# A graph layer and a gated FFN on one core: GpSimd's gathers without a readback, a head that VectorE does alone, and an order planned with other prices

## The reference

```
x = x + gnn(layernorm(x), src, dst, rel)
x = x + ffn(layernorm(x))

gnn:  S = feat[src];  for r in 0, 1: h = relu(relu(S W_r^T + b_r) W_r^T + b_r)    # the one of the edge's relation
      agg = segment_sum(msgs, dst)
      i, g, o of agg W_ih^T + b_ih + b_hh (4 parts, f unused)
      c = sigmoid(i) tanh(g);  hn = sigmoid(o) tanh(c)
      relu(relu(hn W1^T + b1) W2^T + b2) W3^T + b3
ffn:  weights = x wr + br;  the 1561 nodes of highest weight get  (gelu(x w1 + b1) w2 + b2) * weight
      the result of it is added to x for those nodes, for the others x alone
```

## Time and profile before

| | us |
|---|---|
| median of 3 runs | 752.13 |
| lowest, highest | 749.86, 757.51 |
| the profiled execution: its time | 752.0 |
| its span, first to last instruction | 750.2 |
| TensorE busy | 668.3 (89%) |
| VectorE busy | 411.4 (55%) |
| GpSimd busy | 445.9 (59%) |
| ScalarE busy | 234.5 (31%) |

### The profile page before, as it was taken

One profiled execution on the slowest core, in us unless ns is written; L12 is line 12 of the kernel. 1 busy time (PEld: TensorE's weight loads), 2 busy tenths in 40 slices (PEclk: granted clock), 3 DMA queues, 4 the chain that ended last, 5 costly groups with the idle time before them and its releaser, 6 DMA issues.

```text
span 750.2 us, 9583 instructions
## 1 busy us (share of the span) xinstructions
PE 668.3 (89%) x3037; PEld 433.4 (58%) x3037; DVE 411.4 (55%) x1280; ACT 234.5 (31%) x403; POOL 445.9 (59%) x1301
## 2 busy tenths in 40 slices
PE   3978959689999999994857999999999999699986
PEld 2665638456666666653423666565665665377665
DVE  6764987898887988841215035143053244314475
ACT  1243234244333333300312333423414233032601
POOL 3567870376767676767777677647257677760000
PEclk9999979799999999997978999999999999799999
DMA  9300111333323333337333333313123332330005
GB/s 278 95 32 28 56 56 57 98 100 91 104 87 105 89 105 88 97 98 253 94 95 99 92 98 88 94 52 102 44 62 102 91 99 84 107 91 22 1 1 171
DMA packets 37881, 67.63 MB, mean 90 GB/s; under 512 B 7951, under 2 KB 25376, under 8 KB 37824
## 3 DMA queue, kind: packets, MB, share of 16 engines
q0 software_dynamic: 17712, 48.39, 22.0%
q1 hardware_dynamic: 19296, 17.77, 7.3%
q10 hardware_dynamic: 816, 0.79, 0.3%
HBM read 57.17 MB, written 9.75 MB: 89 GB/s over the span
## 4 chain that ended last, share of the span: by engine, by line
PE 75%; DVE 12%; POOL 6%; issue 3%; DMA 2%; ACT 2%; SPq 0%; DVEq 0%; POOLq 0%
PE BIG L1253 21%; PE SM L1397 12%; PE SM L1322 11%; PE AG L1416 10%; PE BIG L1384 6%; POOL ring L1046 5%; PE BIG L1212 4%; PE SM L1223 3%; PE BIG L1276 3%; PE AG L1223 2%; PE BIG L1193 2%; DVE half_b L1530 1%; DVE late L1514 1%; DVE ve L1484 1%; DMA ring<-message_table,rowT 1%
## 5 line engine op out<-in xcount | busy, mean ns | idle before, releaser
L1046 POOL DMA_INDIRECT ring<-message_table,rowT x369 | 366.3, 993 | 158.0 <-issue 106.1
L1416 PE MATMUL AG<-ring,onehot 128*128 128x512 f16 x369 | 95.3, 393 | 29.1 <-DMA ring<-message_table,rowT 25.2
L1322 PE MATMUL SM<-half_b,late 128*128 128x256 f32 x400 | 94.1, 383 | 1.5 <-DVEq L1598 0.8
L1322 PEld LDWEIGHTS SM<-half_b,late 128*128 128x128 f32 x400 | 74.5, 190 | 18.9 <-issue 5.7
L1253 PE MATMUL BIG<-fT,half_a 128*128 128x512 f32 (+1 forms) x192 | 81.4, 579 | 0.0
L1416 PEld LDWEIGHTS AG<-ring,onehot 128*128 128x128 f16 x369 | 41.5, 115 | 67.1 <-DMA ring<-message_table,rowT 16.6
L1253 PE MATMUL BIG<-half_b,half_a 128*128 128x512 f32 (+2 forms) x200 | 73.0, 521 | 0.5 <-ACT half_b L1135 0.5
L1397 PE MATMUL SM<-late,half_a 128*128 128x512 f16 x250 | 70.1, 381 | 0.7 <-ACT half_a L1119 0.7
L1767 DVE TENSOR_TENSOR onehot<-dst,iota_b 128x512 f16<-128x512 f16 (+3 forms) x115 | 45.0, 422 | 43.9 <-PE AG L1416 42.7
L1635 DVE TENSOR_TENSOR late<-late 128x1024 f32<-128x1024 f32 (+2 forms) x7 | 7.8, 1112 | 103.0 <-ACT late L1140 103.0
L1723 DVE TENSOR_SCALAR oh_key<-iota,lists 128x350 f16<-128x350 f16 (+8 forms) x228 | 58.8, 315 | 4.6 <-PE BIG L1384 4.0
(11 more groups left out here) (194 smaller groups left out, 909.8 us busy)
## 6 DMA issues: line engine op xcount, KB each, us to landing
ring<-message_table,rowT POOLq DMA_INDIRECT x369, 2.8
message_table<-late SPq DMA_DIRECT2D x10, 512.0 KB, 3.6
out<-X SPq DMA_DIRECT2D x24, 128.0 KB
X<-in_x SPq DMA_DIRECT2D x4, 512.0 KB, 6.2
half_a<-in_f SPq DMA_DIRECT2D x1, 1024.0 KB, 7.7
half_b<-in_f SPq DMA_DIRECT2D x1, 1024.0 KB, 12.0
message_table<-late SPq DMA_DIRECT2D x2, 384.0 KB, 2.9
half_a<-in_w_ih_t SPq DMA_DIRECT2D x1, 768.0 KB, 4.3
```

Source lines behind the costliest of these rows:

```text
L1046: nc.gpsimd.indirect_dma_start(ring[:, to * W:(to + 1) * W], None, table, bass.IndirectOffsetOnAxis(ap=rowT[:, t:t + 1], axis=0)).then_inc ...
L1322: last = nc.tensor.matmul(bank, hidden_of(s)[:, c, j * P:(j + 1) * P], F2[:, c, :], start=(c == 0), stop=(c == HC - 1))
L1416: mm = nc.tensor.matmul(AG[w % 2][:, :], hot[:, :, i], ring[:, to:to + W], start=(c == FIRST_OF[w] and i == lo), stop=(c == LAST_OF[w] and ...
```

## The change: what it does

- The pauses are gone: GpSimd issues its 369 gathers and waits only for places in the ring. `land` has no term for them.
- Of the head, GpSimd keeps the memsets of the tile constants, in eight batches that wait on the progress of the table and of the layer norms in place of the bias sums, in another order (tile_low first). VectorE takes over the slot rows (`rows_of_slots`, 47 operations after group 1) and the test of the bounds (`compare`, after group 4), which compares tile by tile and reduces a maximum, in place of differences formed on GpSimd. The slot products on TensorE come after group 3, not 4.
- The addition of b3 to X leaves the head (two groups on VectorE, five on GpSimd) and is done by VectorE at the start of `gates(s)`, for each s.
- Seven keys and the rows ahead of them are made before the last group's messages (`EARLY`); the slots of the key ring are renumbered so that these seven lie outside the memory that the messages use.
- TensorE's wait for the whole table moves from ahead of the hot phase to the first dense product and the first visit.
- aggT starts its bank with its first product, without a product of zeros ahead of it.
- The planner's prices are others.

```diff
-    BURST = 7
-    PAUSES = list(range(BURST, NQ, BURST))
...
-                    begin = max(landed[-1] if landed else 120.5, waited[k - RQ] + 3.0 if k >= RQ else 0.0)
-                    landed.append(begin + 1.25 * quad_tiles(k) + (3.0 if k in PAUSES else 0.0))
+                    begin = max(landed[-1] if landed else 126.1, waited[k - RQ] + 3.0 if k >= RQ else 0.0)
+                    landed.append(begin + 1.25 * quad_tiles(k))
...
                 if kind == "tile":
-                    return sum(max(0.06, 0.02 + (hi - lo) * A / 2400) for _, lo, hi in HALVES[s])
+                    return sum(max(0.05, 0.005 + (hi - lo) * A / 2400) for _, lo, hi in HALVES[s])
                 if kind == "dense":
-                    return 0.218 * len(piece(s[1]))
+                    return 0.2145 * len(piece(s[1]))
                 if kind == "down":
-                    return 0.24 * len(down_parts(s[0])[s[2]])
+                    return 0.43 * len(down_parts(s[0])[s[2]])
...
-                return {"aggT": 0.3, "gates": 1.4, "W1": 0.24, "W2": 0.12, "W3": 0.24, "n2T": 0.25, "F1": 0.24}[kind] * nb
+                return {"gates": 2.6, "W1": 0.43, "W2": 0.22, "W3": 0.43, "n2T": 0.27, "F1": 0.43}[kind] * nb
...
-                before = {"gates": ("aggT", 1.6), "W1": ("gates", 5.0), "W2": ("W1", 1.1), "W3": ("W2", 1.1), "n2T": ("W3", 7.5)}
+                before = {"gates": ("aggT", 1.7), "W1": ("gates", 3.1), "W2": ("W1", 0.9), "W3": ("W2", 0.9), "n2T": ("W3", 5.5)}
...
-                now += 0.06 + 0.24 * (hi - lo)
+                now += 0.03 + 0.2145 * (hi - lo)
...
             for i in range(BATCHES):
-                pool.wait_ge(summed, i + 1)
+                if i % 2 == 0:
+                    pool.wait_ge(lows_done, start_of(i // 2 + 1))
+                else:
+                    pool.wait_ge(feat_ready, i // 2 + 3)
...
-                if s in PAUSES:
-                    pool.wait_ge(gathered[(s - 1) % RQ], landed_at(s - 1))
-                    for i in range(12):
-                        last = nc.gpsimd.memset(pause_out[:, i, :], 0.0)
-                    last.then_inc(paused, 1)
-                    pool.wait_ge(paused, PAUSES.index(s) + 1)
...
-                        nc.tensor.matmul(b[:, 0:n], zeros16[:, :], iota16[:, 0:n], start=True, stop=False, skip_group_check=True)
                         for i, (part, pick_of, lo, hi) in enumerate(parts):
-                            last = nc.tensor.matmul(b[:, lo:hi], part[:, c * P:(c + 1) * P], pick_of, start=False,
+                            last = nc.tensor.matmul(b[:, lo:hi], part[:, c * P:(c + 1) * P], pick_of, start=(i == 0),
...
+            def rows_of_slots():
+                dve.wait_ge(big_free, at[("big", "spread", 3)] + 1)
+                for j, (t, c, nodes) in enumerate(WINS):
+                    first, k = min(a for a, _ in nodes), slots_of(nodes)
+                    last = nc.vector.tensor_scalar(slot_row[:, SLOT0[j]:SLOT0[j] + k], iota16[:, 0:k], tmin_b[:, c:c + 1],
+                                                   float(first), ALU.add, ALU.add)
+                last.then_inc(slots_ready, 1)
...
+            def compare():
+                dve.wait_ge(bounds_set, N_BOUNDS)
+                nc.vector.tensor_tensor(low_t[:, 0:TH], low_t[:, 0:TH], tile_low, ALU.max)
+                step(nc.vector.scalar_tensor_tensor(far, tmax_b[:, 0:TH], float(HOT * P - 1), tile_low, ALU.min, ALU.subtract))
+                nc.vector.tensor_tensor(far, far, width_t, ALU.is_ge)
+                nc.vector.tensor_tensor(tmin_b, tmin_b, low_t, ALU.is_lt)
+                step(nc.vector.tensor_tensor(tmax_b, tmax_b, high_t, ALU.is_ge))
+                step(nc.vector.tensor_tensor(tmin_b, tmin_b, tmax_b, ALU.max))
+                step(nc.vector.tensor_tensor(tmin_b[:, 0:TH], tmin_b[:, 0:TH], far, ALU.max))
+                step(nc.vector.tensor_reduce(bad[:, :], tmin_b, AX.X, ALU.max))
...
             def gates(s):
                 n = blocks(s) * P
+                t, k = start_of(s), blocks(s)
+                nc.vector.tensor_tensor(X[:, t:t + k, :], X[:, t:t + k, :],
+                                        b3[:, :].unsqueeze(1).broadcast_to([P, k, D]), ALU.add)
```

More of the change, by code:

```diff
@@ L651, in chosen_time @@
         def chosen_time(s):
[L652 removed]
+            return sum(max(0.31, (hi - lo) * 4 / 2400) for o, _, lo, hi in CHOSEN if o == s) * KC
         def schedule():
@@ L886, in build @@
             full_at[("big",) + key] = sum(1 for k in big_items[:n + 1] if k[0] != "window")
+        EARLY = min(i for i, (kind, n) in enumerate(vector_steps) if kind not in ("key", "rows") or
+                    (kind == "key" and n >= MORE_KEYS))
         block = ctx.enter_context(nc.Block())
@@ L997, in _ @@
-            pool.wait_ge(weights_in, 16 * N_LOADS)
-            for s in range(2, NS):
-                t, n = start_of(s), blocks(s)
-                pool.wait_ge(feat_ready, s + 1)
-                nc.gpsimd.tensor_tensor(X[:, t:t + n, :], X[:, t:t + n, :],
-                                        b3[:, :].unsqueeze(1).broadcast_to([P, n, D]), ALU.add).then_inc(biased, 1)
             pool.wait_ge(plan_ready, 1)
```

132 lines of the change are left out of this document (51 added, 81 removed).

## The result

| | before | after |
|---|---|---|
| median (runs beside each other) | 751.0 (4 runs) | 707.84 (4 runs, 706.25 to 708.52) |
| profiled execution, its span | 752.0, 750.2 | 708.52, 706.7 |
| mean granted clock | 0.956 | 0.981 |

A forecast was written before the change was run, and what follows sets the result against it. TensorE bounds two long stretches, the gather stream the gap behind the hot phase. Gains of 14 (2 + 13 - 1) there, 3 for zero fills and 8 at 640 took 752.0 less 25 to 727, stated as 726; range 704 to 748.

The forecast's parts named there:

- rival 1: Gap behind the hot phase no longer gather-bound, shrinks to its work, 25 in place of 14 us: 712; chance 0.2.
- the sum's second one, the head: Before the hot phase: VectorE relieved of held-up operations, first gather 2 us sooner, hot phase 4 us sooner.
- the place at 640: Short TensorE gap at 640 to 653 us and slowed work after; new prices to gain 8 of 9.5 us.
- the walk along VectorE: VectorE's order in the head, added 10.4 + 3.5 us against removed waits, additions, slot products: hot phase moves by 4 us.
- the bound of +8: Upper bound on the hot phase's move in the head, if no VectorE operation is held up at all.
- The readback: Gather stream: each pause costs 2.2 us, six ahead of tile 186 give 13 us; every gather then takes 1.30 us.
- The gap is bound by gathers: Stretch from 337 to 403 us, behind the hot phase: takes the gathers' gain, 2 + 13 - 1 = 14 us.
- Rivals 2 and 4: Readback's cost returns, 1.38 us a gather, 743, chance 0.2; gathers queue up and slow, 766 at 1.50 us, chance 0.1.
- rival 3: Head lengthens by 6 us through slot rows and comparison on VectorE, gathers start 6 late: 734; chance 0.05.
- The bias additions beside gathers: VectorE additions at gates steps stretch the gather beside them by 0.97: -1 us before tile 186, -5 in all.
- Zero fills: 14 products of zeros into the aggT banks go, 0.22 us each, 3 us on TensorE's path.
- The order: Old prices ask for chunks too early in the hot phase, too late beside fixed work; new ones gain 8 us.

The follow-up runs named there:

- b_no_pauses: The kernel before without its readbacks, order and head untouched: 730.82 us, ratio 0.9711.
- a_old_prices: The kernel after, its order planned with the old prices, first gather priced at 126.1, no term for pauses: 719.51 us, ratio 0.9563.
- a_bias_pool: The kernel after with the seven additions of b3 to X back on GpSimd in the head: 713.51 us, ratio 0.9473.
- a_no_early: The kernel after without keys ahead of the last two blocks' messages: 706.52 us, ratio 0.939.
- a_pauses: The kernel after with the thirteen readbacks put back, order untouched: 741.93 us, ratio 0.9834.
- b_new_prices: The kernel before, its order planned with the new prices, its own pause term and landing start kept: 745.04 us, ratio 0.9919.
- b_both: The kernel before without readbacks and with the new prices, on a chip where everything was 100 us slower: 854.88 us, ratio 1.0182.

## Why it came out so, step by step

**The forecast** of 726 lies 18 us above the result. Its sign and its range held, the range only by the lower end of 704 that rival 1 had set, for a mechanism that didn't come, and so by luck. One chain of kernels leads from before to after, with more changed at each step (spans of the profiled executions):

| step | forecast | span | gain |
|---|---|---|---|
| kernel before | | 750.2 | |
| without readbacks (b_no_pauses) | 13 | 728.6 | 21.6 |
| head, bias additions, zero fills, landing times of the plan (a_old_prices) | 2 - 1 + 3 = 4 | 717.9 | 10.7 |
| prices (kernel after) | 8 | 706.7 | 11.2 |

The step that failed is the sum's second one, the head (below). The first was too small because the place at 640 belongs to the readbacks, and the third has its size for another reason than the one given.

**The head: 4 us forecast for the hot phase and 2 for the gathers, 17.6 and 15.6 measured.** The step that failed is the walk along VectorE, "Removed: the 3.3 + 3.6 us of held-up operations, 2.4 us of two bias additions", and with it the bound of +8. By the timelines of before and after, TensorE's products of the messages run ahead as follows:

| products that begin | before | after | sooner | what lies between |
|---|---|---|---|---|
| first half, third group | 59.98 | 51.72 | 8.3 | VectorE: two layer-norm operations, 4.53 and 3.28 us, take 0.88 each; TensorE's waits behind them, 3.88 and 3.04 us, become 0.22 and 0.72 (6.0); 16 products behind the first wait 5.16 us, then 3.62 (1.5); 0.6 from before |
| second half, fourth group | 84.00 | 74.55 | 9.4 | the products behind the wait at 59.98 were slower (9.4 us to 69.35; 7.8 us from 51.72 to 59.54 after); 0.4 lost again behind |
| second half, fifth group | 108.03 | 93.17 | 14.9 | the wait of 8.76 gone; 2.06 of slot products and 1.92 of waiting added |
| second half, sixth group | 123.97 | 105.68 | 18.3 | 5.04 us become 3.62; the slot products no longer here |
| last ones of the second half | 134.33 | 117.81 | 16.5 | a wait of 1.52 behind the comparison |
| first hot product | 140.38 | 122.77 | 17.6 | early keys |

I made four mistakes in it. I left out one of the two layer-norm operations that the train of memsets holds up (4.53 us). I walked VectorE and didn't ask where TensorE stood for it. For the 8.76 us wait, which a_bias_pool brings back with the additions, there was a single row of the trace, and VectorE was late for it because of its operations from 82.67 to 103 us (tile lows 10.38 where 8.31 are enough, messages 4.98, 1.24 and 0.97 where 1.47, 0.69 and 0.68 are enough). These lengthenings are 6.4 us; what else there was of the wait, the slot products and the wait of 1.92 us fill in the kernel after. I set the hidden slot rows half on the path; they are wholly hidden (VectorE ends them at 61.64, TensorE stands nowhere for them, and the second operation behind them waits 0.96 us for TensorE). And I took off 2.4 us for two bias additions that were hidden too. In the kernel before they begin after the third group's products have begun, and VectorE is idle after them:

```profile
59.98 8.66 PE L1212 MATMUL BIG<-fT,WR 128*128 128x512 f32 x16 [3.04 <-ACT ring L1103]
...
60.96 2.36 DVE L1565 TENSOR_TENSOR X<-X,b 128x1024 f32<-128x1024 f32 x2
71.28 0.69 DVE L1509 TENSOR_TENSOR oh_key<-SM,onehot 128x512 f32<-128x512 f32 x1 [7.96 <-PE SM L1223]
```

By the runs that undo one part of the head each, the first gather is 8.0 us later for the bias additions on GpSimd and the first hot product 0.8 for the trains; no run undoes the rest alone. What I had added for VectorE was right in size: slot rows 8.8 us (10.4 forecast), comparison 7.0 (7 forecast). Of the early keys I said that they add to the gain of the hot phase; a_no_early shows 0.7 us there at most and nothing in the time.

**The readback: 13 us for six, measured 16.4 for the same stretch.** The six steps at readbacks sum to 21.8 us (3.49, 3.66, 3.47, 3.47, 3.51, 4.19) in place of 7.8, which is 14.0; two slow steps of 2.52 and 2.62 us that the kernel after doesn't have make up the rest. The one of 2.62, right behind the fourth readback, stands there in a_pauses and b_new_prices too. "I take 1.30 us for every gather" is 1.302 measured, and the bursts go on without end. The readbacks alone were worth 21 us with the old order and 33 in the new one, so the seven late ones, which the sum put at nothing, weren't free either: 7.4 us behind the first F1 product with the old order, 14.6 with the new one.

**The gap is bound by gathers.** Right between these two kernels: its end moved by 34.3 us, of which 32.1 are the 186th gather's, and both orders visit 184 tiles ahead of the first F1 product. It isn't the whole of it, since with the old prices and nearly the same gathers the end lies 12.4 us later (a_old_prices). The waits that are left end on gathers except the last, 3.34 us for the layer norm. Rival 1 gave nearly the right time (712) for another reason: the gap's idle time shrank to 13 us and not to nothing. Rivals 2 and 4 fell with the spacing, rival 3 with the head.

**The bias additions beside gathers: 1 us ahead of the first F1 product and 5 in all forecast.** In the kernel after the seven additions lie at 329.38, 370.62, 445.44, 498.19, 554.29, 610.15 and 647 us. The gathers beside them take up to 1.52 us instead of 0.95 and are some 2 us longer in all, 0.6 of it at 329.94.

**Zero fills and the place at 640: 3 + 8 = 11 forecast, 9.1 measured**, of which 5.3 are busy time of TensorE (12 fills and the clock) and 3.7 idle time. The size is right and the reason for the 8 us is not: the sum has them from the new prices. The stretch from the first F1 product to the end shrinks by 7.4 us when the readbacks go (b_no_pauses). When the prices change it grows by 1.1, some 3 us of additional visits included (b_new_prices). For the 349 tiles of the sixth group TensorE doesn't stand, as forecast, but at 607 it stands 3.25 and then 0.77 us for the last tiles.

**The order.** Right in direction from both sides, 7 and 12 us against the 8 that I gave it, but the place is another: the 9.64 us wait ahead of the first group's aggT, which the prediction named as the old prices' fault and gave no price, and the chain of steps behind it. Its price of 1.25 us for a gathered tile is too low against 1.302, 19 us over 369 tiles; whether a better one gains is open.

**Parts don't add.** Undone one at a time in the kernel after, readbacks (33), prices (12), bias additions (6) and slot rows (up to 8) come to 58, more than the 43.5 of all together, while put in one at a time into the kernel before they give 21 and 7. As I read it, a part that makes gathers sooner is worth its full size only when the order asks for them and nothing else is late; b_both, which was to show it, can't be read.

## What to carry to other kernels

When two engines slow each other, price the removal of one's work by the waits of the engine that sets the end (here one wait of 8.76 us), and then by the twins of the held-up operations over the whole stretch, not by the rows that look long. When a stretch is bound by a stream, every us of its start and of its spacing counts up to the last item that somebody waits for, and an engine that waits 29 us for places in the ring has an order behind it that asks too late. Measure a part from both ends, added to the old kernel and removed from the new one, before quoting what it is worth, and look where in the timeline its time comes out: here the prices gave about what was expected of them, and none of it at the place that was to give it.

## What the runs showed of the hardware that I had not expected

- 369 gathers of 128 rows follow each other at 1.30 us without any readback and don't slow down.
- A VectorE operation on four columns that takes 0.17 us alone took 4.53, 3.28 and 3.26 us beside trains of memsets 34 ns apart and ended within 0.03 us of each train's last memset; two others ended in the middle of a train, right behind a memset of 114 or 83 columns. The layer norm's statistics operations beside the same memsets (0.39 to 0.42 us, from 53.58 to 55.62 in the kernel before) weren't held up.
- One gather stood 20.26 us with a DMA share of 0.01. The Trainium skill (SBUF — State Buffer, SBUF: two separate sides) describes that GpSimd can't write a DMA's descriptors while certain VectorE instructions run. The low DMA share would fit, but in the kernel after VectorE is as full in the same stretches (10.00 of 10 us) and the gathers go on, so this case doesn't show that it is the same thing.
- On one chip TensorE, VectorE and ScalarE stood together for up to 8.2 us with no instruction as releaser in the trace while GpSimd issued gathers, 34 to 43 us in all; the kernel before took 100 us more there than on the other chips. What holds them was not found.
